# Values folded before the first LN chain, the last outputs of the lag attention one sum at a time, the last LN inside the quantised stage, and its scales written once

## The reference

```python
x = x + jnp.tanh(g_xattn[0]) * _L0_xattn_ref(_layernorm(x), ctx_4096, ctx_4096)      # lag attention
x = x + jnp.tanh(g_ffn[0]) * _L0_ffn_ref(_layernorm(x), gate_w, u, g, d)             # 16 experts, top 2
x = x + jnp.tanh(g_xattn[1]) * _L1_xattn_ref(_layernorm(x), ctx_4096, Wq, bq, Wk, bk) # context attention
x = x + jnp.tanh(g_ffn[1]) * _L1_ffn_ref(_layernorm(x), ...)                         # quantised FFN
```

```python
scale = jnp.maximum(jnp.max(jnp.abs(xs), axis=-1, keepdims=True) / QMAX, 1e-08)
q = jnp.clip(jnp.round(xs / scale), -QMAX, QMAX)
```

## Time and profile before

| | us |
|---|---|
| median of 3 runs | 1393.91 (1393.74 to 1394.57) |
| the profiled execution | 1396.99 |
| its span (all times below are in it) | 1395.3 |
| PE busy | 1260.5 (90%) |
| PEld busy | 855.8 (61%) |
| DVE busy | 783.5 (56%) |
| POOL busy | 577.7 (41%) |
| ACT busy | 501.7 (36%) |
| lag attention ends, route stage starts | 447.2, 448.3 |
| context attention ends, quantised stage starts | 1216.0, 1220.05 |

### The profile page before, as it was taken

One profiled execution on the slowest core, in us unless ns is written; L12 is line 12 of the kernel. 1 busy time (PEld: TensorE's weight loads), 2 busy tenths in 40 slices (PEclk: granted clock), 3 DMA queues, 4 the chain that ended last, 5 costly groups with the idle time before them and its releaser, 6 DMA issues. The chain is left out here.

```text
span 1395.3 us, 20860 instructions
## 1 busy us (share of the span) xinstructions
PE 1260.5 (90%) x6492; PEld 855.8 (61%) x6498; DVE 783.5 (56%) x2009; ACT 501.7 (36%) x875; POOL 577.7 (41%) x957
## 2 busy tenths in 40 slices
PE   3899999999976999999999998999999999558786
PEld 1354454545433955448888786989888888334443
DVE  2878888888774572005533333443545442359995
ACT  2544444444431600013322222332222232078884
POOL 4676877868653000003312121423321221158885
PEclk9999999999997999999999999999999999889998
DMA  5120211502000900416777874526323330121111
GB/s 192 65 91 31 90 60 33 192 15 85 36 0 17 348 1 1 148 59 239 252 257 264 272 238 154 181 92 158 100 91 106 121 110 12 60 68 46 60 60 76
DMA packets 52481, 156.38 MB, mean 112 GB/s; under 512 B 5952, under 2 KB 16192, under 8 KB 52288
## 3 DMA queue, kind: packets, MB, share of 16 engines
q1 hardware_dynamic: 39152, 113.60, 22.8%
q0 software_dynamic: 13264, 41.95, 10.5%
HBM read 113.06 MB, written 45.61 MB: 114 GB/s over the span
## 5 line engine op out<-in xcount | busy, mean ns | idle before, releaser
L1197 PEld LDWEIGHTS ex_bank<-ex_xT,ex_gu 128*112 128x112 f32 x1248 | 140.4, 177 | 25.2 <-issue 24.2
L1197 PE MATMUL ex_bank<-ex_xT,ex_gu 128*112 128x128 f32 x1248 | 143.8, 273 | 2.6 <-issue 1.7
L44 PE MATMUL xa_bank<-fT_high,M_hi 128*128 128x256 f32 x512 | 143.8, 281 | 0.0
L46 PE MATMUL xa_bank<-fT_high,M_lo 128*128 128x256 f32 x512 | 142.8, 279 | 0.0
L45 PE MATMUL xa_bank<-fT_low,M_hi 128*128 128x256 f32 x512 | 142.7, 279 | 0.0
L52 PE MATMUL la_bank<-la_osum,la_tab 128*128 128x512 f32 x256 | 121.7, 620 | 15.9 <-POOL la_osum L297 14.6
L297 POOL TENSOR_TENSOR la_osum<-la_oprod 128x512 f32<-128x512 f32 x64 | 80.1, 1273 | 96.4 <-DVE la_oprod L476 96.4
L1061 POOL TENSOR_TENSOR ex_small<-listed,ex_small 128x1 int32<-128x1 int32 x42 | 15.4, 366 | 224.9 <-DVE Wk L1139 224.8
L44 PEld LDWEIGHTS xa_bank<-fT_high,M_hi 128*128 128x128 f32 x512 | 96.7, 189 | 0.3
L52 PE MATMUL la_bank<-la_v_raw,la_tab 128*128 128x512 f32 x128 | 65.6, 637 | 34.6 <-POOL la_v_raw L267 19.8
L46 PEld LDWEIGHTS xa_bank<-fT_high,M_lo 128*128 128x128 f32 x512 | 96.6, 189 | 0.0
(11 more groups left out here) (281 smaller groups left out, 2846.8 us busy)
## 6 DMA issues: line engine op xcount, KB each, us to landing
produced<-Wk SPq DMA_DIRECT2D x39, 512.0 KB, 4.1
ex_gu<-in_gate_up SPq DMA_DIRECT2D x16, 896.0 KB, 7.0
X<-in_x SPq DMA_DIRECT2D x8, 1024.0 KB, 7.2
la_v_raw<-in_ctx SPq DMA_DIRECT2D x16, 512.0 KB, 4.0
produced<-la_zeros SPq DMA_DIRECT2D x16, 512.0 KB, 4.7
normal<-rt_xn SPq DMA_DIRECT2D x16, 512.0 KB, 5.7
fT<-in_ctx_T SPq DMA_DIRECT2D x8, 1024.0 KB, 5.5
xa_f<-in_ctx SPq DMA_DIRECT2D x8, 1024.0 KB, 4.8
```

The lines of the kernel that those rows point to most:

```text
L44: pe.matmul(out, a[0], b[0], start=first, stop=False)
L46: return pe.matmul(out, a[1], b[0], start=False, stop=last)
L1197: m = pe.matmul(bank[half][0:INTER, 0:P], gu[:, slot, at:at + INTER], xT[:, k, :], start=(k == 0), stop=(k == KD - 1))
```

## The change

Five edits:

1. Lag attention, POOL: the first folds of the values go ahead of the first LN chain, the first folds of the queries right behind it, then the memset of `zeros`. The step that did both folds returns at once.
2. Lag attention, TensorE: for the last unit `last_positions` takes the place of `positions(u, 0)` and `positions(u, 1)`. It waits for two sums, multiplies the first for both banks, then the second, and so on.
3. Context attention: DVE's `variance` and POOL's `on_pool` of the last batch are left out. In the quantised stage DVE makes the variance first of all, POOL prepares the constants before the pipeline and makes the chain ahead of its product of tile 2, and ACT waits for it before tiles 14 and 15 and in each step of the loop.
4. Quantised stage: `scale_now` and `scale_h_now` go. The scale is written once, into `scale_x` and `scale_h`, and the reciprocal reads that slice.
5. Between each wait for the scale and the reciprocal there is a memset of one column (`spare`).

```diff
@@ lag_attention, gpsimd
-            norm.on_pool(pool, 0)
-            pool.memset(zeros[:], 0.0).then_inc(s["zeroed"], 1)
...
+            v_halves(0, 0, 0)
+            norm.on_pool(pool, 0)
+            q_halves(0)
+            pool.memset(zeros[:], 0.0).then_inc(s["zeroed"], 1)
+
             def step(on, due):
                 before2, before, now, after, next2 = on(-2), on(-1), on(0), on(1), on(2)
+                if next2 and isinstance(next2[0], int) and next2[0] == 0:
+                    return
@@ lag_attention, tensor
+            def last_positions(u):
+                for i in range(4):
+                    at_least(pe, s["osums"], 4 * u + max(i + 1, 2))
+                    for j in range(2):
+                        m = full_product(pe, bank[4 + j][:], pos_t(i, j), osum[:, i, :], i == 0, i == 3)
+                        if i == 3:
+                            m.then_inc(s["out_pe"], 1)
+
             def step(on, due):
                 before, now, after = on(-1), on(0), on(1)
+                if before and not now:
+                    last_positions(before[0])
+                    return
@@ context_attention, gpsimd and vector
-                after.on_pool(pool, b)
+                if b + 1 < B:
+                    after.on_pool(pool, b)
...
-                dve.wait_ge(s["added"], 4 * b + 4)
-                after.variance(dve, X, b)
+                if b + 1 < B:
+                    dve.wait_ge(s["added"], 4 * b + 4)
+                    after.variance(dve, X, b)
@@ quantised_ffn
+        norm.signal_with(sem)
...
             pool.dma_start(w_d[:].rearrange("p (k n) -> p k n", k=KH), w_down_T.rearrange("(k p) n -> p k n", p=P)).then_inc(s["w_d_in"], 16)
+            norm.prepare(pool)
...
                 a, m, e = on(2), on(0), on(-2)
+                if isinstance(a, int) and a == 2:
+                    norm.on_pool(pool, B - 1, 0)
...
                     at_least(act, s["xu_ready"], a)
+                    if not isinstance(a, int) or a >= TILES - 2:
+                        act.wait_ge(norm.ready, 1)
...
         def _(dve):
+            norm.variance(dve, X, B - 1, 0)
...
-                    dve.tensor_scalar(scale_x[:, bass.ds(a, 1), :].rearrange("p o c -> p (o c)"), peak[:], 1.0 / QMAX, 1e-8, ALU.mult, ALU.max)
-                    dve.tensor_scalar(scale_now[:], peak[:], 1.0 / QMAX, 1e-8, ALU.mult, ALU.max).then_inc(s["chain"], 1)
+                    scale_now = scale_x[:, bass.ds(a, 1), :].rearrange("p o c -> p (o c)")
+                    dve.tensor_scalar(scale_now, peak[:], 1.0 / QMAX, 1e-8, ALU.mult, ALU.max).then_inc(s["chain"], 1)
                     dve.wait_ge(s["chain"], 3 * a + 3)
-                    dve.reciprocal(inv_x[:], scale_now[:]).then_inc(s["scale_ready"], 1)
+                    dve.memset(spare[:], 0.0)
+                    dve.reciprocal(inv_x[:], scale_now).then_inc(s["scale_ready"], 1)
...
-                    dve.tensor_scalar(scale_h[:, bass.ds(m, 1)], peak_h[:], 1.0 / QMAX, 1e-8, ALU.mult, ALU.max)
-                    dve.tensor_scalar(scale_h_now[:], peak_h[:], 1.0 / QMAX, 1e-8, ALU.mult, ALU.max).then_inc(s["hchain"], 1)
+                    dve.tensor_scalar(scale_h[:, bass.ds(m, 1)], peak_h[:], 1.0 / QMAX, 1e-8, ALU.mult, ALU.max).then_inc(s["hchain"], 1)
                     dve.wait_ge(s["hchain"], 2 * m + 2)
-                    dve.reciprocal(inv_h[:], scale_h_now[:]).then_inc(s["scale_h"], 1)
+                    dve.memset(spare[:], 0.0)
+                    dve.reciprocal(inv_h[:], scale_h[:, bass.ds(m, 1)]).then_inc(s["scale_h"], 1)
```

More of the change, by code:

```diff
@@ L1624, in quantised_ffn @@
         q = [sb("q_g", [P, KD, P], BF16), sb("q_u", [P, KD, P], BF16)]
-        peak, scale_now, inv_x = (sb(n, [P, 2]) for n in ("peak", "scale_now", "inv_x"))
+        peak, inv_x = (sb(n, [P, 2]) for n in ("peak", "inv_x"))
         scale_x = sb("scale_x", [P, TILES, 2])
@@ L1630, in quantised_ffn @@
         hq = sb("hq", [P, HIDDEN])
-        peak_h, scale_h_now, inv_h = (sb(n, [P, 1]) for n in ("peak_h", "scale_h_now", "inv_h"))
+        peak_h, inv_h = (sb(n, [P, 1]) for n in ("peak_h", "inv_h"))
+        spare = sb("spare", [P, 1])
         scale_h = sb("scale_h", [P, TILES])
```

## The result

| | before | after |
|---|---|---|
| median of the runs, first comparison | 1394.24 (1393.74 to 1395.98) | 1375.61 (1374.20 to 1376.49) |
| median of the runs, second comparison | 1393.67 (1391.78 to 1397.20) | 1378.93 (1376.43 to 1380.35) |
| span of the profiled execution | 1395.3 | 1374.6 |
| PE, DVE, POOL busy | 1260.5, 783.5, 577.7 | 1259.7, 779.1, 579.4 |

The ratio is 0.9868, interval 0.9847 to 0.9890, in the first comparison: 18.6 us by the medians, 18.4 by the ratio, 20.6 by the two spans (1395.25 and 1374.61 unrounded), where the forecast was 17.8. A second comparison, run with the experiments, gave 0.9884 (0.9868 to 0.9900): 16.2 us by the ratio, 14.7 by the medians. No engine does noticeably less: what changed is who waits.

The account below looks back on a forecast made before the run. The prediction took serial hand-overs between engines to bound the kernel, no engine having more than 6% of the chain. Terms 3.3 + 3.3 + 9.1 + 2.1 = 17.8 us took the median from 1393.9 to 1376.1, range 1370.5 to 1381.5.

Parts of the forecast that it names:

- Values folded first: Lag attention's start: value products from about 9.9 us, query products at 20.4, correlation at 27.9 to 29.2; gain 3.3 us.
- The doubt kept for the range: TensorE at 43.7 to 49 us: half speed after a 2.80 us idle may vanish; 2.6 us, left out of the sum.
- Last outputs: Lag attention's end: TensorE starts on the second of four sums, 2.72 us earlier; gain 3.3 us, bounds 1.5 and 6.0.
- my mean of four places: Last outputs of the lag attention: low-rate stretch taken as 4.9 us, so 16 records take 9.3 us instead of 10.14.
- Last LN: Between context attention and quantised stage: 1.05 us remains after the last add; gain 9.1 us, bounds 6.15 and 9.1.
- near 1180: Sign of being right: POOL's drain at the context attention's end near 1180 us, under 1.5 us from last add to next stage.
- Scales once: Quantised stage: a single scale instruction avoids being caught behind POOL's product; gain 2.1 us, bounds 3.2 and -0.9.
- two catches at 1.1 each: Quantised stage: second scale instruction caught by POOL in 2 of 16 tiles; 1.1 us for the last, 1.1 for the other.
- Rival 1: Clock luck: no half-speed stretch at 43.7 us (2.6) and last outputs at full speed (2.7): 1370.8 us; chance 0.14.
- Rival 2: End of context attention: POOL's drain must be waited for wherever it starts, only 6.15 us gained: 1379.1 us; chance 0.10.
- rival 3: Quantised stage: the scales bring nothing, register work takes the gain back, caught both times: 1378.2 to 1379.1 us; chance 0.20.
- rival 4: Quantised stage: new memsets and reciprocals are caught by POOL too, 38 us come in: 1414 us, slower; chance 0.02.

Follow-up runs that it names:

- o_single_columns: Changed kernel with the two-column scale instruction of the quantised stage split into two of one column each: 1374.40 us, ratio to before 0.9854.
- e1_values: Kernel before with only the first part, values folded ahead of the LN chain and query folds directly behind it: 1391.98 us, ratio 0.9979.
- f_late_pool: Changed kernel with one more small POOL instruction that waits for the context attention's last add: 1381.23 us, ratio to before 0.9895.
- e4_scales: Kernel before with only the fourth part, each scale written once and a small memset ahead of each reciprocal: 1394.77 us, ratio 0.9997.
- e2: Also e2_outputs: kernel before with only the second part, the lag attention's last products each waiting for their own sum: 1392.56 us, ratio 0.9980.
- e3: Kernel before with only the third part, the last batch's variance and LN chain made in the quantised stage: 1386.05 us, ratio 0.9930.
- m_undo_scales: Changed kernel without its fourth part, each scale written twice again: 1380.73 us, ratio to before 0.9899.
- l_three_columns: Changed kernel with a third, constant column in peak, scale and inverse, so the scale instruction has three columns: 1376.77 us, ratio to before 0.9868.

## Why the prediction was right

**What bounds it: right, but not by the row that was read first.** In each of the four places a wait on the path became shorter, and the stretches show it. The chain of the earlier trace rows does not: it reaches back only to 1220.05, the start of the quantised stage, and its shares add up to the 12% that this stage has of the span. That no engine has more than 6% of it says nothing of the other stages; the timelines carried the step.

**Values folded first: 3.3 predicted, 2.3 to 4.2 measured, mean 3.1.** The first product (9.9 said, 9.82 came) and the query products (20.4, 20.21) held. The first correlation came between 27.67 and 29.54 in the ten profiles with this part, a little beyond both ends of the 27.9 to 29.2 that was said; POOL's sums were the limit in three of them, after among them. By the pace of the records the low stretch after the restart was some 3 us in after and 6 in o_single_columns. The doubt kept for the range, half speed behind 40 us, was sized right: from the first to the second correlation it is 18.65 us in before, 17.66 in after and 15.96 in e1_values, where all of the 2.6 us came in.

**Last outputs: 3.3 predicted, 2.7 to 4.3 measured.** The start on the second sum held everywhere. The term hung on the length of the low stretch; my mean of four places could not be better than the scatter, since the same kernel gave 3.34 and 2.75. That after, with its 3.34, meets the 3.3 is in part luck.

**Last LN: 9.1 predicted, 9.15 measured,** in all kernels that have it, and 3.2 us come back in f_late_pool. Variance and chain cost nothing in the next stage, within 0.3 us. That POOL's transfers make the drain long was a correlation of two rows. The route stage with a transfer has since shown 3.3 and 4.0 us, which ended with the landing; for the 2.84 a price of 0.082 us for each of the block's transfers fits, as an estimate. The term did not need it: it went by where the drain starts, and that is shown. The drain began at 1188.33; "near 1180" was a slip, as 1196.1 less the 6.6 us of the first two terms is 1189.5.

**Scales once: 2.1 predicted, 2.0 in the two spans, 1.0 to 2.4 by the stage's length, 0.4 by e4_scales.** That the two spans met the sum was luck: it was hit by other terms than mine. I took the per-tile cost at 0 and two catches at 1.1 each. In fact each steady tile saves 0.07 us (the -0.06 end of my bound, nine tiles, 0.6 us), the last tile's catch is in before and e1_values but not in e2, e3 and m_undo_scales, so that the 0.9 us behind the last scale are chance of this pair, and the early tiles give the rest. The Trainium skill, "VectorE: DVE Perf Modes", section "Rules for kernel authors", advises to minimise the number of operations; here the number stayed the same and a steady tile became 0.07 us shorter, so that advice did not decide.

**The step that was too coarse** is the price of chance. The sum was made against one execution, and an untouched stretch alone moves the span by 3.1 us. The range of 11 us (1370.5 to 1381.5) was wide enough for both medians, 1375.6 and 1378.9; the forecast's 17.8 lies between the two comparisons, 18.6 and 14.7 by the medians. Rival 1 was half right: the half-speed stretch behind 40 us was shorter (by 1.0 us of its 2.6 in after, and gone in seven of the ten profiles with this part), and the last outputs did not find full speed. It is not the change that removes it: e2_outputs, with the start of before, did not have it either. Rival 2 is ruled out by the seam, rival 3 by the stage's lengths, rival 4 by the memset's 0.06 us in every tile.

## What to carry to other kernels

At a stage's end, look which queue ends last and what drains behind it: moving 6 us of work into the next stage's idle start gained 9 us, because the drain of the queue that had issued 34 transfers no longer came last. A two-column tensor_scalar on DVE beside POOL's work can cost what POOL's instruction has left; one-column forms were free, and then the loop's next wait shows. Judge a part of some 2 us by the length of its own stretch in several profiles, and not by the kernel's median.

## What the runs showed of the hardware

DVE instructions held up until POOL's product ended: tensor_scalar of 128x2 (1.00 us instead of 0.17) and 128x3 (1.04), scalar_tensor_tensor of 128x2 with both sources in SBUF (1.00). Not held up beside such a product: tensor_scalar of 128x1 (0.15), reciprocal of 128x2 (0.16), the reductions, the memset (0.06), and all with a source in PSUM. The Trainium skill, "SBUF — State Buffer", section "Who interferes with whom", names both held kinds: two-port modes, and two inputs in SBUF against a GpSimd instruction that reads SBUF. The page "VectorE: DVE Perf Modes" of the Trainium skill, section "Mode 2×_2P", adds the condition for the two-port mode: an even outermost dimension, or an odd one that is equal in source and destination. By it three columns are held as two are, against my theory for l_three_columns, and the runs agree. For a single element the page decides nothing, and the runs show it free.

After an idle of 2.76 to 2.80 us the same four products of TensorE took 1.98 us (e1_values, e2_outputs), 2.50 (e4_scales), 2.99 (after) and 3.78 (before): nearly the same gap, and from no half speed to all of them at half speed. Of the 14 profiles eight had 1.98. The rows of before, e1_values and after stand above and in the earlier trace rows; the granted clock in these windows is 1.00 for e1_values and 0.57 for after.

```profile
41.00:44.00 3.00, 2.40 (x6) 0.76 (x4) 2.96 (x8) 1.48 (x4) 1.98 (x2) 1.00 0.01 3
```

```profile
40.00:44.00 4.00, 3.98 (x6) 1.18 (x4) 3.82 (x14) 0.80 (x2) 3.10 (x3) 0.57 0.01 2
```
